# A gated cross-attention block with top-1 experts: the softmax's sum over keys reads the last key tile from its buffer, and the orders of the engines are written anew

## What is computed

```python
h = layernorm(x)                                   # (8, 512, 512)
Q, K, V = h @ Wq.T + bq, ctx @ Wk.T + bk, ctx @ Wv.T + bv
scores = einsum('bhqd,bhkd->bhqk', Q, K) / sqrt(32)
attn = softmax(scores, axis=-1)                    # over 512 keys
x = x + tanh(g0) * ((attn @ V) @ Wo.T + bo)
probs = softmax(layernorm(x) @ router_w + router_b)
x = x + tanh(g1) * max(probs) * (layernorm(x) @ expert_w[argmax(probs)] + expert_b[argmax(probs)])
```

## Time and profile before

| what | value |
|---|---|
| median of 3 runs | 1189.92 us |
| the profiled execution | 1192.07 us, span 1190.3 us |
| mean granted TensorE clock | 0.956 |
| TensorE busy | 1094.6 us, 92% of the span |
| VectorE busy | 759.0 us, 64% |
| GpSimd busy | 667.2 us, 56% |
| ScalarE busy | 563.0 us, 47% |

### The profile page before, as it was taken

How to read it: one execution, slowest core, us unless ns; L and a number is a source line. 1 busy time by engine, 2 the same in 40 slices (tenths; PEclk the granted TensorE clock), 3 DMA queues, 4 the chain that set the end, 5 groups by cost and what they waited for, 6 DMA issues and landing times.

```text
span 1190.3 us, 19122 instructions
## 1 busy us (share of the span) xinstructions
PE 1094.6 (92%) x5464; PEld 709.2 (60%) x5464; DVE 759.0 (64%) x1620; ACT 563.0 (47%) x1016; POOL 667.2 (56%) x446
## 2 busy tenths in 40 slices
PE   2798999999999999999999999999999996898996
PEld 1564467556755675567556655575557642786774
DVE  4645545766576657665765677556765665778654
ACT  4145643564356435644564356445644456423431
POOL 3046645764576457645764576545764555644662
PEclk9798999999999999999999999899999986699998
DMA  6233323423343334333332342233332319324541
GB/s 230 62 77 102 82 72 80 113 80 81 79 121 80 81 77 119 82 79 89 111 79 72 79 120 72 73 80 111 86 81 73 83 53 321 127 95 147 166 140 54
DMA packets 70885, 119.39 MB, mean 100 GB/s; under 512 B 17854, under 2 KB 18878, under 8 KB 70656
## 3 DMA queue, kind: packets, MB, share of 16 engines
q1 hardware_dynamic: 62496, 98.96, 30.2%
q0 software_dynamic: 6240, 18.68, 5.0%
q10 hardware_dynamic: 2048, 0.53, 0.2%
HBM read 50.42 MB, written 18.66 MB: 58 GB/s over the span
## 4 chain that ended last, share of the span: by engine, by line
PE 68%; DVE 13%; issue 6%; ACT 5%; POOL 3%; DMA 3%; DVEq 1%; ACTq 0%; SPq 0%; POOLq 0%
PE jb L459 10%; PE jb L460 9%; PE jb L461 9%; PE sc L482 8%; PE jb L502 8%; PE hb L492 8%; DVE maxima L836 6%; PE sc L664 5%; ACT probs L688 3%; PE jb L602 2%; PE jb L515 2%; POOL psum_keys L1095 2%; PE jb L530 1%; PE jb L594 1%; PE hb L650 1%
## 5 line engine op out<-in xcount | busy, mean ns | idle before, releaser
L836 DVE TENSOR_REDUCE maxima<-jb 128x1 f32<-128x512 f32 x512 | 321.7, 680 | 112.2 <-PE jb L502 110.8
L688 ACT ACTIVATE probs<-sc 128x512 f32<-128x512 f32 x512 | 285.4, 598 | 190.5 <-PE sc L482 153.8
L1095 POOL TENSOR_TENSOR psum_keys<-psum_keys,probs 128x1024 f32<-128x1024 f32 x128 | 302.6, 2384 | 110.7 <-ACT probs L688 110.6
L1095 POOL TENSOR_TENSOR psum_keys<-probs 128x1024 f32<-128x1024 f32 x64 | 151.8, 2383 | 231.3 <-ACT probs L688 230.9
L502 PE MATMUL jb<-k_stack,q_stack 96*128 96x512 f32 x512 | 188.4, 435 | 19.1 <-issue 4.9
L482 PE MATMUL sc<-q_stack,k_stack 98*128 98x512 f32 x512 | 190.7, 435 | 14.9 <-ACT probs L688 11.5
L482 PEld LDWEIGHTS sc<-q_stack,k_stack 98*128 98x128 f32 x512 | 94.4, 192 | 107.6 <-ACT probs L688 56.0
L502 PEld LDWEIGHTS jb<-k_stack,q_stack 96*128 96x128 f32 x512 | 92.6, 190 | 110.4 <-issue 51.2
L492 PE MATMUL hb<-probs,values 128*32 128x512 f32 x1024 | 139.3, 628 | 3.4 <-ACT probs L688 2.5
L459 PE MATMUL jb<-c_hi,wk_hi 128*128 128x512 f32 x128 | 52.4, 409 | 15.4 <-POOL c_lo L1099 15.4
L664 PE MATMUL sc<-e_hi,heads_hi 128*128 x156 | 65.9, 422 | 0.5 <-DVE heads_raw L1067 0.5
(11 more groups left out here) (226 smaller groups left out, 1958.6 us busy)
## 6 DMA issues: line engine op xcount, KB each, us to landing
k_stack<-k_hi SPq DMA_DIRECT2D x256, 64.0 KB, 2.0
q_stack<-q_hi SPq DMA_DIRECT2D x256, 64.0 KB, 2.0
stage<-in_x SPq DMA_DIRECT2D x63, 256.0 KB, 2.9
stage<-in_ctx_t SPq DMA_DIRECT2D x32, 256.0 KB, 3.0
k_stack<-k_lo SPq DMA_DIRECT2D x128, 64.0 KB, 2.0
q_stack<-q_lo SPq DMA_DIRECT2D x128, 64.0 KB, 2.0
e_lo<-in_ew SPq DMA_DIRECT2D x8, 1024.0 KB, 14.0
rows<-row SPq DMA_DIRECT2D x30, 257.5 KB, 3.0
```

Of the source, the lines that this page charges most:

```text
L688: nc.scalar.activation(probs[:, kt % 2, h, :], scs[(16 * g + n) % NSC][:], ACT.Exp, scale=SCALE)\
L836: nc.vector.tensor_reduce(maxima[g % 2][:, n:n + 1], jbs[j][:], AX.X, ALU.max).then_inc(s["mx_done"], 1)
L1095: nc.gpsimd.tensor_tensor(psum_keys[:, two, :], in0, probs[:, kt % 2, two, :], ALU.add)\
```

## The change

`SUM` reads key tiles 0 to 2 from `psum_keys` and adds tile 3 in PSUM by four more matmuls that read `probs[:, 1]`. GpSimd's additions `A4` and `A5` are no longer in the tables. All counts of `acc_done` go from 6 to 4 a group. The exponentials of key tile 1, which overwrite `probs[:, 1]`, wait for the `SUM` of the group before.

```diff
 elif kind == "SUM":
-    pe.wait_ge(s["acc_done"], 6 * (g + 1))
+    pe.wait_ge(s["acc_done"], 4 * (g + 1))
+    pe.wait_ge(s["exp_done"], 16 * (g + 1))
     jb_free(j)
     for h in range(HG):
-        last = nc.tensor.matmul(jbs[j][h * HD:(h + 1) * HD, :], ones[:], psum_keys[:, h, :],
-                                start=True, stop=True)
+        nc.tensor.matmul(jbs[j][h * HD:(h + 1) * HD, :], ones[:], psum_keys[:, h, :], start=True, stop=False)
+    for h in range(HG):
+        last = nc.tensor.matmul(jbs[j][h * HD:(h + 1) * HD, :], ones[:], probs[:, 1, h, :], start=False, stop=True)
 elif kind == "E":
-    wait(act, s["acc_done"], 6 * g + (h2 + 1 if kt >= 2 else 2 * kt - 4 + h2 + 1))
+    if kt == 1:
+        wait(act, s["sum_mm"], g)
+    else:
+        wait(act, s["acc_done"], 4 * g + (h2 + 1 if kt >= 2 else h2 - 1))
```

The tables are written anew. In TensorE's part of `ORDER`, around the four `SUM`s and in the stretch with the maxima of group 2:

```diff
-1MT Vc3 Vd3 0P2 0P3 2M0 2M1 ~RL0 0SUM 1S0 2M2 3Q 1S1 3Qb 3Qc 3Qd 1S2 0SC 1S3 2M3 3K 1S4 1S5 1S6 3Kb 3Kc ~RC0
-2M4 3Kd 1S7 1S8 1S9 1P0 1S10 1S11 2M5 1P1 1S12 2M6 2M7 2M8 2M9 2M10 1S13 ~LI0 2M11 2M12 2M13 2M14 2M15 1S14
-1P2 1P3 2S0 2S1 2S2 2S3 1SUM 3M0 3M1 3M2 2S4 2S5 1SC
-2P3 3S0 3S1 3S2 3S3 2SUM 3S4 3S5 3S6 3S7 2SC 3P0 ^0M0
-^0S0 ^0S1 ~RC1 3P3 ^Vb1 ^0S2 ^0S3 ^Vc1 ^Vd1 ^V2 ^Vb2 ^Vc2 ^Vd2 ^1M0 ^1M1 ^1M2 ^0S4 3SUM
+0P2 0P3 1MT ~RT1 2M0 0SUM 2M1 ~RL0 2M2 2M3 3Q 3Qb 1S0 1S1 3Qc 1S2 1S3 0SC 3Qd 1S4 1S5 1S6 3K ~RC0 3Kb 3Kc
+3Kd 2M4 1S7 1P0 2M5 1S8 1S9 2M6 1S10 2M7 2M8 2M9 1S11 2M10 1S12 2M11 1S13 1P1 2M12 2M13 2M14 2M15 1S14
+1P2 ~OPc3 ~OPd3 0NM 1P3 2S0 2S1 2S2 1SUM 2S3 2S4 3M0 3M1 2S5 1SC
+2P3 3S0 3S1 3S2 2SUM 3S3 3S4 3S5 3S6 3P0 2SC ^0M0
+^0S0 ~RC1 3SUM ^0S1 ^0S2 ^Vb2 ^0S3 ^Vc2 ^Vd2 3P3 ^1M0 ~LI1
```

`LI0` moves behind `2MT` on TensorE, and on VectorE behind `2M15`. ScalarE's `2SUM` moves from behind `3E4` to behind `3E5`, its `2OU` from in front of `3E0` to behind it. In the opening:

```diff
 SP
-LW1 ^DC0 ^DC1 ^DC2 LW0 ^DC3 ^DX0 LC LW2 LW3 ^DX1 ^DX2 ^DX3 ^0SK ~RW2 ~RW3 ^0SQ
+LW1 ~RW2 ^DC0 ^DC1 ^DC2 LC ^DC3 ^DX0 LW0 LW2 ^DX1 ^DX2 ^DX3 LW3 ^0SK ^0SQ ~RW3
 ACT
-WT0 WT1 WT2 WT3 ^C0 ^C1 TH WT4 ^C2 WT5 ^C3 ^0K ^NX0
+^C0 ^C1 WT0 ^C2 WT1 TH WT2 WT3 WT4 ^C3 ^NX0
```

For the last batch VectorE's end of `ORDER` changes (ScalarE's `W0 W1 3OU W6 W2 3SUM` becomes `W0 3SUM 3OU W1 W6 3SC W2`), and `DR1`, the load of a residual tile, moves to the head of the next table:

```diff
-W0 ~LI1 PA 3SC W1 PC 3NM 3NL W6 W2 OP0 LR0 OP1
+W0 3SC ~LI1 PA W1 PC W6 3NM 3NL OP0 W2 LR0 OP1
```

More of the change, by code:

```diff
@@ L50 @@
     "SP": [
-        "~~RW2 1SQ 1SK ^DC0 ~~RW3 2SQ 2SK ^DC1 ^DC2 ~RW0 ~RW1 ^DC3 ~DR2 ~DR3 ^DX0 3SQ ^DX1 3SK ^DX2 ^DX3 DR0 DR1",
+        "~~RW2 ~~RW3 ~DR1 1SQ 1SK 2SQ 2SK ^DC0 ^DC1 ^DC2 ~RW0 ~RW1 ^DC3 ~DR2 ~DR3 3SQ ^DX0 ^DX1 3SK ^DX2 ^DX3 DR0",
         "^0SQ ^0SK",
@@ L54 @@
     "PE": [
[11 rows of a table removed]
[11 rows of a table added]
     ],
     "ACT": [
[6 rows of a table removed]
[6 rows of a table added]
     ],
     "DVE": [
[6 rows of a table removed]
[6 rows of a table added]
     ],
     "POOL": [
-        "~LR0 1A0 ^C0 1A1 ^C1 ^C2 ^C3 1A2 ~OP2 ~OP3 1A3 1A4 1A5 ~LR1 ^LX0 ^LX1 2A0 2A1 ^LX2 ^LX3 2A2 2A3 2A4 2A5",
-        "OP0 OP1 3A0 3A1 3A2 3A3 3A4 3A5 ^0A0 ^0A1 ^0A2 ^0A3 ^0A4 GA0 ^0A5",
+        "~2A1 LX2 LX3 ~~LR1 ~2A2 ~2A3 ~3A0 ~3A1 ~3A2 ~3A3 0A0 0A1 ~OP0 ~OP1 0A2 0A3 ~LR0 1A0 ^C0 1A1 ^C1 ^C2 1A2",
+        "~OP2 ~OP3 ^C3 1A3 ^LX0 2A0 ^LX1",
     ],
@@ L90 @@
     "SP": [
-        "LW1 ^DC0 ^DC1 ^DC2 LW0 ^DC3 ^DX0 LC LW2 LW3 ^DX1 ^DX2 ^DX3 ^0SK ~RW2 ~RW3 ^0SQ",
+        "LW1 ~RW2 ^DC0 ^DC1 ^DC2 LC ^DC3 ^DX0 LW0 LW2 ^DX1 ^DX2 ^DX3 LW3 ^0SK ^0SQ ~RW3",
     ],
     "PE": [
[5 rows of a table removed]
[5 rows of a table added]
     ],
     "ACT": [
[3 rows of a table removed]
[4 rows of a table added]
     ],
     "DVE": [
[4 rows of a table removed]
[3 rows of a table added]
     ],
     "POOL": [
-        "^C0 ^C1 ^C2 ^C3 ^LX0 ^LX1 ^LX2 ^LX3 ^0A0 ^0A1 ^0A2 ^0A3 ^0A4 ^0A5",
+        "^C0 ^C1 ^LX0 ^C2 ^C3 ^LX1",
     ],
@@ L117 @@
     "SP": [
-        "~~RW2 ~DR2 W0 ~~RW3 W1 W6 W2 W3 W4 W5 W7 ~DR3 EB ~RW0 ~RW1 ~RW2 ~RW3",
+        "~DR1 ~~RW2 ~~RW3 ~DR2 W0 W1 W6 W2 W3 W4 W5 W7 ~DR3 EB ~RW0 ~RW1 ~RW2 ~RW3",
     ],
@@ L828, in item @@
                     wait(dve, s["exp_done"], 16 * g + HG * kt + 2 * h2 + 2)
-                    wait(dve, s["acc_done"], 6 * g + n - 1)
+                    wait(dve, s["acc_done"], 4 * g + n - 1)
                     nc.vector.tensor_tensor(psum_keys[:, two, :], psum_keys[:, two, :], probs[:, kt % 2, two, :], ALU.add)\
@@ L1014, in item @@
                     wait(dve, s["pv_done"], NT * NG * B)
-                    wait(dve, s["acc_done"], 6 * NG * B)
+                    wait(dve, s["acc_done"], 4 * NG * B)
                     wait(dve, s["rc_free"], 2 * B)
@@ L1092, in item @@
                     else:
-                        wait(pool, s["acc_done"], 6 * g + n - 1)
+                        wait(pool, s["acc_done"], 4 * g + n - 1)
                         in0 = psum_keys[:, two, :]
@@ L1128, in item @@
                     wait(pool, s["pv_done"], NT * NG * B)
-                    wait(pool, s["acc_done"], 6 * NG * B)
+                    wait(pool, s["acc_done"], 4 * NG * B)
                     wait(pool, s["fin"], n + 1 - SLOTS)
```

## The result

The kernel after takes 1204.88 us (median of 4 runs, 1203.14 to 1208.04), the kernel before 1189.43 in runs beside it (4 runs): ratio 1.013 [1.0101, 1.0158]. The change makes it 1.3% **slower**, by 15.5 us. The forecast was 1186.3 us and the other sign; the time lies inside the range, near its upper end.

A forecast was written before the change was run, and what follows sets the result against it. It took TensorE, busy 92% of the span, as the bound, with stalls that could swallow new work. 27.5 - 11.4 - 8.9 - 7.8 - 3.0 = -3.6 gave 1186.3 us; range 1174 to 1207, 8 times in 10.

The forecast's parts named there:

- The price on TensorE: Four more matmuls in each SUM cost about 0.86 us; over 32 groups +27.5 us if all on the path.
- The price off TensorE: GpSimd loses 152.6 us of additions, by itself worth nothing; the new waits between sums and exponentials cost 0.
- 2SUM: The larger SUM of group 2 fills TensorE's stall for an exponential, leaving it 0.56 us better: -11.4 us over 8 batches.
- 1SUM: At group 1's SUM the price is hidden in 8 batches and maxima start 0.4 us earlier in 5: -8.9 us.
- 0SUM and 3SUM: The SUMs of groups 0 and 3 stand on the chain, so 16 x 0.86 us stays, already in the 27.5.
- Maxima of group 2: Moving LI0 out from between group 2's maximum matmuls removes the whole 1.11 us gap in 7 batches: -7.8 us.
- Opening: At the kernel's start, earlier context tile work and small loads cut TensorE's idle time: -3.0 us.
- End: At the last SUM, the added matmuls and the vanished wait for GpSimd's addition come to net near 0.
- (C): Rival: the hold moves, GpSimd's additions holding line 915 or 944; up to 10.0 us more, 1196.3 us; chance 0.05.
- (A): Rival: TensorE pays everywhere, the stalls at 1SUM and 2SUM only shifting later; +16.7, 1206.6 us; chance 0.14.
- What would show it: Signs to check, among them a batch's period: 118.7 us before, 118.6 forecast, 121.2 by (A); 2 or more longer, absorption failed.

The follow-up runs named there:

- the kernel with the step put back: The kernel after with only RS0 (ScalarE) and RG0 (VectorE, ahead of 0SC again) moved back: ratio to the kernel before 0.996, in a second run 0.9974 (1185.70 us).
- K's split first: The kernel after with RS0 and RG0 put back, and VectorE taking 3K ahead of 2M4: 1188.58 us, ratio 0.9986 to the kernel before.
- the first two experiments: The kernel before's tables without A4 and A5: first with the change's larger SUM, ratio 1.0151; then with only four matmuls, last key tile left out, 0.9956.

## Why the prediction was wrong

The sum was -3.6, the profiled execution had +13.75. By the prediction's own steps:

- **The price on TensorE** was right: 0.86 a `SUM`, measured from start to start and as the difference of two kernels (0.86, 0.86, 0.8, 0.9). All 32 paid are 27.4 us, against the 27.5 written.
- **The price off TensorE**, 0, was right as far as seen: line 519 waits for nothing, and line 517's matmuls wait 1.4 us for GpSimd, 1.2 before.
- **2SUM** (absorbed, and 0.56 a batch better) was right. The third and fourth stretch together give -0.1 us in an even batch, where the 0.86 of `3SUM`, less 0.56, less the 0.47 of `1MT` and `~RT1` would be -0.2. The experiment that moves the two sums shows the mechanism: ahead of the score matmul that waits it costs nothing, behind it 0.86, though there only in half of the batches.
- **1SUM** (absorbed, and 2.0 us better in all) was right in the absorption: 27.11 us with four matmuls and with eight. The 0.4 better in five batches came out at 0.3 in four; in batch 4, where line 915 hadn't been held before, the stretch is 0.4 longer (26.73 to 27.11). That the sum over six batches is -2.5 is luck, since 1.6 of it is one batch of the kernel before at a lower clock.
- **0SUM and 3SUM**: paid, as written.
- **Maxima of group 2** is the step that failed. It said -7.8, the whole gap in 7 batches, with 0 as its worst end. The gap did go: with `RG0` put back the stretch takes 31.43 us, and 31.10 + 0.86 + 0.47 - 31.43 = 1.00 us a batch of the gap of 1.11 is gone. But in the kernel after the stretch came out at +20.1 us for six batches, of which `0SUM`'s price is 6 x 0.86 = 5.2 and `1MT` and `~RT1` are 2.8, so the step gave **+12.1**. Its six stretches take 208.2 us, and six of 31.43 are 188.6: what took the gain back cost 19.7 us (16.0 in the second trace of the same kernel). It stood in the same rewritten table of VectorE from which I read `LI0`'s move: `RG0` stands behind `3K`, meets GpSimd's addition, and holds the maxima for 1.17 us; and the clock falls, at 1.2 to 2.5 us more.
- **Opening** failed as well, at a smaller price: -3.0 was predicted, +0.6 came up to the first `0P3`. The wait for the small load went, and TensorE's third K step starts at 17.58 and no longer at 18.27, but 4.31 of the 4.99 us of idle time are still there:

```profile
9.00 0.61 ACT L742 ACTIVATE c_hi<-stage 128x512 fp32r<-128x512 f32 x1
15.08 0.95 POOL L1110 TENSOR_TENSOR rt<-rt,tiny 128x1 f32<-128x1 f32 x1 [4.11 <-DVE rt L882]
16.27 1.26 POOL L1105 TENSOR_TENSOR c_lo<-stage,c_hi 128x512 fp32r<-128x512 f32 x1
16.95 0.63 ACT L746 ACTIVATE wq_hi<-probs 128x512 fp32r<-128x512 f32 x1 [5.68 <-DMA probs<-in_wq_t]
17.58 0.79 PE L460 MATMUL jb<-c_hi,wk_hi 128*128 128x512 f32 x1 [4.31 <-POOL c_lo L1105]
```

ScalarE's half of the third context tile is done at 9.61, as the prediction wanted it. But GpSimd's table was rewritten too: `^LX0`, which waits for VectorE's statistics of the first x tile, now stands ahead of `^C2`, so GpSimd's half, and TensorE behind it, wait for that. The prediction didn't look at GpSimd's part of the opening. The fourth tile is hardly earlier than before, 19.47 for 19.93, for another reason: `WT4` stands ahead of `^C3` in ScalarE's queue, and waits 5.68 us for `Wq`, whose later request the working named ("Wq is asked for after DX0") without following it to the item behind. The opening and the end were not tried by themselves.

- **End**: 0 was written; the last batch has +1.3 and what follows it -3.2, so near it.

Of the rivals, **(C)** had the mechanism and named line 944, at a chance of 0.05. Its price was a hold of 1.43 us in 7 batches, 10.0 above the forecast. The hold itself was so sized (1.17 measured). But it was priced as if it cost its own length alone, and it lay where TensorE starves and the clock falls; before, line 915's hold had cost only 0.7 us a batch. And "whatever instruction is hit" was too wide, as the reciprocal beside line 950 shows. (A)'s test, a period 2 us or more longer, came true (734.5 / 6 = 122.4 against 120.2 for the mean of batches 1 to 6) for another reason than (A)'s: the experiment with four matmuls in the new tables has the same loss.

Without the failed step the forecast itself comes out: 1186.3 us is 0.997 of the kernel before, and the kernel with the step put back has 0.9974 and 0.996. An even batch of it takes 118.6 us (31.44 + 27.11 + 60.02), as "What would show it" has it. The steady part was thus sized rightly; that the whole agrees is luck too, since the opening's 3.0 didn't come.

## What to carry to other kernels

When a table of orders is written anew, look at each small VectorE instruction that moves, and ask what GpSimd runs at the place to which it goes: a 0.2 us instruction can take the whole rest of a 2.4 us one, and everything queued behind it waits too. Not every instruction is held (the reciprocal beside it wasn't), and a hold costs only where the path runs through it: 0.79 us in `~RG1` cost nothing, 1.17 in `~RG0` cost itself and the clock. When an item moves, follow also what other engines' queues have behind its result, as the load behind `~RW0`. Price the matmuls added to a full TensorE by their place: directly ahead of the one that waits they can be free, directly behind it they are paid. And read the clock of each stretch beside its length before putting a loss down to work, since here the step put back was worth 3.3 us a batch in the first pair of traces (208.2 / 6 = 34.7 against 31.43) and 2.7 in the second, of which the hold's own length is 1.17 and the rest came with the fallen clock.

## What was unexpected of the hardware

- A stretch of 32 us in which TensorE waits once for some 1.2 us was granted the full clock in some batches and 0.95, 0.90 or 0.86 in most, with the same work: 32.57, 33.8, 35.1 and 36.6 us. The clock comes down shortly after the wait (the `P` at 469.97 at half speed), and gives a loss as large as the wait or larger. It also fell where nothing was held: in three of six batches with K's split first, where the wait for `k_lo` was only 0.49 us, and in three of six in each of the first two experiments. So the wait alone doesn't decide it, and what does stays open.
- The hold by GpSimd doesn't depend on the form of the VectorE instruction as far as tried: `tensor_scalar` on 128 x 2 elements took 1.40 us for 0.23, `tensor_tensor` 1.38 for 0.164, each to within 0.03 us of the addition's end. A reduction and a reciprocal on as few elements weren't held beside the same addition.
- The chips differ by more than the changes: 1190 and 1207 us for the same kernel, so that only ratios from one chip say anything here.
